# Expert token lists on four column strips of TensorE, and a new order of gather and scatters on GpSimd

## What is computed, cut to what matters

```python
capacity = max(1, int(Sz * CAP_FACTOR / E) + 1)          # 313 of 1250 tokens for each of 8 experts
scores = softmax(x @ router_w.T)
gate_vals, sel_idx = top_k(scores.T, capacity)
tokens = x[sel_idx]                                      # gather
h = gelu(tokens @ w1 + b1)                               # 1024 -> 512
y = h @ w2 + b2                                          # 512 -> 1024
out = zeros_like(x).at[sel_idx].add(y * gate_vals)       # scatter with add
x = x + out
```

## Time and profile before

| what | value |
|---|---|
| median of 3 runs | 1496.85 us (1491.33 to 1496.93) |
| the profiled execution: own time | 1494.7 us |
| its span in the profile | 1492.8 us |
| mean granted clock of TensorE | 0.982 of full |
| instructions | 28252 |
| PE, PEld, DVE, ACT, POOL busy | 1420.1, 727.0, 884.3, 545.5, 357.1 us |
| read from and written to memory | 118.40 MB, 41.94 MB |

### The profile page before, as it was taken

The page is one execution under the profiler, slowest core; times in us unless marked ns, Lnnn a source line. Parts: engine busy times, 40 slices in busy tenths (PEclk is TensorE's granted clock), DMA queues, the critical chain, the costliest instruction groups (busy, mean ns, idle before and its releaser), DMA issues.

```text
span 1492.8 us, 28252 instructions
## 1 busy us (share of the span) xinstructions
PE 1420.1 (95%) x8351; PEld 727.0 (49%) x8351; DVE 884.3 (59%) x1994; ACT 545.5 (37%) x758; POOL 357.1 (24%) x373
## 2 busy tenths in 40 slices
PE   6789999999999999999999999999999979999996
PEld 5344444545444444444654444446544436566653
DVE  7788888686987887541342222223337686576652
ACT  4578757373624543210111210001111124565651
POOL 4332320202201110000874002800012311343232
PEclk9999999999999999999999999999999987999998
DMA  7242010000166565553323443530046645789963
GB/s 282 43 86 51 8 43 14 28 0 28 70 193 168 162 167 174 144 144 108 130 72 88 98 111 113 183 105 22 0 130 197 196 177 205 217 249 273 281 164 57
DMA packets 156675, 185.96 MB, mean 125 GB/s; under 512 B 106172, under 2 KB 107659, under 8 KB 156600
## 3 DMA queue, kind: packets, MB, share of 16 engines
q1 hardware_dynamic: 144440, 143.07, 31.4%
q0 software_dynamic: 12160, 41.95, 11.0%
HBM read 118.40 MB, written 41.94 MB: 107 GB/s over the span
## 4 chain that ended last, share of the span: by engine, by line
PE 74%; DVE 11%; issue 6%; ACT 3%; DMA 2%; DVEq 1%; POOL 1%; ACTq 0%; SPq 0%; POOLq 0%
PE ps L1344 31%; PE ps L1412 11%; PE ps L1567 7%; PE ps L1587 6%; PE ps L1244 3%; PE ps L1246 3%; PE ps L1245 3%; PE ps L1175 2%; PE ps L1593 1%; PE ps L1555 1%; ACT th L1671 1%; DVE hm L2048 1%; PE ps L1273 1%; PE ps L1202 1%; PE ps L1236 1%
## 5 line engine op out<-in xcount | busy, mean ns | idle before, releaser
L1344 PE MATMUL ps<-wa,tb 128*128 128x512 f16 x960 | 212.2, 383 | 4.1 <-issue 4.1
L1412 PE MATMUL ps<-adj,nm 128*128 128x384 f16 (+2 forms) x960 | 169.6, 340 | 1.6 <-DVEq L2363 1.6
L1244 PE MATMUL ps<-gp,hop 128*128 (+1 forms) x400 | 151.6, 379 | 1.0 <-DVE gn L2122 1.0
L1344 PEld LDWEIGHTS ps<-wa,tb 128*128 (+1 forms) x960 | 94.1, 99 | 118.4 <-issue 9.4
L1245 PE MATMUL ps<-gp,hop 128*128 (+1 forms) x400 | 151.6, 379 | 0.0
L1246 PE MATMUL ps<-gp,hop 128*128 (+1 forms) x400 | 151.6, 379 | 0.0
L1412 PEld LDWEIGHTS ps<-adj,nm 128*128 x960 | 93.9, 98 | 77.2 <-issue 2.1
L1781 ACT ACTIVATE tb<-cx 128x384 f32 (+1 forms) x48 | 26.8, 559 | 276.8 <-DVE cx L2353 276.8
L1344 PE MATMUL ps<-wa,hop 128*128 128x512 f16 x480 | 105.3, 379 | 2.9 <-DVEq L2297 2.9
L1567 PE MATMUL ps<-tkT,wb 128*128 128x314 f16 x768 | 105.4, 300 | 0.8 <-ACT tkT L1854 0.8
L1344 PE MATMUL ps<-wb,hop 128*128 128x512 f16 x480 | 105.4, 383 | 0.0
(11 more groups left out here) (397 smaller groups left out, 2216.1 us busy)
## 6 DMA issues: line engine op xcount, KB each, us to landing
w_st<-in_ew SPq DMA_DIRECT2D x16, 2048.0 KB, 11.3
self_d<-cr SPq DMA_DIRECT2D x20, 512.0 KB, 3.0
cr<-self_d SPq DMA_DIRECT2D x20, 512.0 KB, 3.3
stage<-in_wn POOLq DMA_DIRECT2D x16, 512.0 KB, 3.8
x_d<-cr SPq DMA_DIRECT2D x10, 512.0 KB, 4.6
cx<-x_d SPq DMA_DIRECT2D x10, 512.0 KB, 4.0
cr<-x_d SPq DMA_DIRECT2D x10, 512.0 KB, 4.2
out<-cr SPq DMA_DIRECT2D x10, 512.0 KB, 3.5
```

The lines of the kernel that those rows point to most:

```text
L1244: pe.matmul(acc, wh, gh, start=(s_ == 0), stop=False, skip_group_check=True)
L1344: ins = pe.matmul(ps[:, b + c, :], lhs(part, k), w[:, w_, k, c * 512:(c + 1) * 512], start=(k == 0 and part == 0 and w_ == 0), stop=(last ...
L1412: ins = pe.matmul(ps[:, 6 + j, 0:n], nm[:, part, s_, bass.ds(f * P, P)], adj[:, s_, t0 * TP:t0 * TP + n], start=first, stop=(s_ == NT - 1 ...
```

## The change

Lists for experts 2 to 7 are computed the other way round. `tokg` of a tile (32 columns: 8 experts by 4 numbers) becomes the weights, on one of four 32-column strips of PE, and `selm` of the tile (384 columns) the moving data: 10 matmuls, tiles 0 to 3 on strips 0 to 3, tiles 4 to 7 again, tiles 8 and 9 on strips 0 and 1. The four strips' partial sums lie on 128 partitions of PSUM bank 0. ACT copies them as halfwords to `strip_lists` (`strips_out`), after it has applied the gates of chunk 0. PE's new `slots`, which stands in `ffn2` behind chunk 1, adds them up and turns them with 3 matmuls against a constant 0/1 matrix `strip_sum`. DVE's `lists` moves behind `out` 1. On POOL the gather moves from ahead of the scatter's chunk 0 to between its chunks 0 and 1. Two small POOL instructions at the program's start make `strip_sum`.

```diff
--- before.py
+++ after.py
@@ -260,6 +260,7 @@
         ones16 = sb("ones16", [P, P], F16)
         one32 = sb("one32", [1, 1], F32)
         sel = sb("sel", [P, 4, 8], F32)
+        strip_sum = sb("strip_sum", [P, 2, 4 * NE], F16)
         stage = sb("stage", [P, 2, 1024], F32)
         sc = sb("sc", [TP, NT, 8], F32)
         marks = sb("marks", [TP, NT, 2, 8], F16)
@@ -469,6 +470,8 @@
         selm = spare[:, 0:NT * 3 * P].rearrange("p (t n) -> p t n", t=NT)
         eb2 = spare[:, NT * 3 * P:NT * 3 * P + 4 * D].bitcast(F32).rearrange("p (j n) -> p j n", j=2)
         eb2t = spare[:, NT * 3 * P + 4 * D:NT * 3 * P + 6 * D].bitcast(F32).rearrange("p (j n) -> p j n", j=2)
+        strips_at = NT * 3 * P + 6 * D
+        strip_lists = spare[:, strips_at:strips_at + 3 * P]
         gE.close()
 
         w1b = wb[:].rearrange("p r (a k) n -> p r a (k n)", a=2)
@@ -541,6 +544,7 @@
         TURN_C, TURN_N, TURN_D = ([TURN_B[j] + 32 * (NT // 2) * n for j in range(2)] for n in (1, 2, 3))
         late = (NT - 2) // 2
         s_tick, s_wsh = sem("s_tick"), sem("s_wsh")
+        s_strips, s_stripped = s_candT, s_row
 
         def rows(ap, t, n=1):
 
@@ -685,6 +689,9 @@
             g.memset(pp[:, :, 16:32], 0.0)
             strips = ident[:].rearrange("p (q n) -> p q n", q=4)
             link(g.tensor_tensor(sel[:], strips[:, :, 0:8], strips[:, :, 8:16], ALU.add))
+            link(g.tensor_tensor(strip_sum[:], ident16[:, 0:64].rearrange("p (a n) -> p a n", a=2),
+                                 ident16[:, 64:128].rearrange("p (a n) -> p a n", a=2), ALU.add))
+            link(g.tensor_tensor(strip_sum[:, 0], strip_sum[:, 0], strip_sum[:, 1], ALU.add))
             g.sem_inc(s_rest, 1)
 
             uses = [0, 0]
@@ -862,9 +869,11 @@
                     g.indirect_dma_start(out=gx[0:n, j, c, :], out_offset=None, in_=h_d[:, :],
                                          in_offset=bass.IndirectOffsetOnAxis(ap=idx[0:n, j, c:c + 1], axis=0)).then_inc(s_gx[j][c], 16)
 
-            def scatter(i, j):
+            def scatter(i, j, between=none):
                 e = 2 * i + j
                 for c in range(3):
+                    if c == 1:
+                        between()
                     g.wait_ge(s_yg, 3 * e + c + 7)
                     g.sem_inc(s_tick, 1)
                     g.indirect_dma_start(out=out_d[:, :] if c < 2 else out_d.rearrange("n (o d) -> (n o) d", o=2),
@@ -875,9 +884,7 @@
                 g.sem_inc(s_scd, 1)
 
             def body(i, j, more):
-                if more:
-                    gather(i + 1, j)
-                scatter(i, j)
+                scatter(i, j, (lambda: gather(i + 1, j)) if more else none)
 
             for j in range(2):
                 g.wait_ge(s_h[j], 16 * (NT // 2))
@@ -1530,11 +1537,23 @@
                     return
                 pe.wait_ge(s_sel, e - 1)
                 pe.wait_ge(s_eev, 6 * e + 2)
+                pe.sem_inc(s_tick, 1)
+                for t in range(NT):
+                    q = t % 4
+                    ins = pe.matmul(ps[32 * q:32 * q + 32, 0, 0:3 * P], tokg[:, t].rearrange("p e n -> p (e n)"), selm[:, t, :],
+                                    start=(t < 4), stop=(t >= NT - 4), skip_group_check=True, tile_position=(0, 32 * q))
+                    if t >= NT - 4:
+                        ins.then_inc(s_strips, 1)
+
+            def slots(i, j):
+                e = 2 * i + j
+                pe.wait_ge(s_stripped, e)
+                pe.sem_inc(s_tick, 1)
+                of = strip_sum[:, 0].rearrange("p (e n) -> p e n", n=4)
                 for c in range(3):
-                    for t in range(NT):
-                        ins = pe.matmul(ps[:, 0, 4 * c:4 * c + 4], selm[:, t, c * P:(c + 1) * P],
-                                        tokg[:, t, e, :] if isinstance(e, int) else tile_of(tokg[:, t], e),
-                                        start=(t == 0), stop=(t == NT - 1))
+                    ins = pe.matmul(ps[:, 0, 384 + 4 * c:388 + 4 * c], strip_lists[:, c * P:(c + 1) * P],
+                                    of[:, e, :] if isinstance(e, int) else tile_of(of, e),
+                                    start=(c == 0), stop=(c == 2), skip_group_check=True)
                 ins.then_inc(s_lst, 1)
 
             def turn(i, j):
@@ -1569,7 +1588,7 @@
                                             stop=(k == KT - 1 and w_ == 1))
                     ins.then_inc(s_f1, 1)
 
-            def ffn2(i, j, between=none):
+            def ffn2(i, j, between=none, behind=none):
                 e = 2 * i + j
                 pe.wait_ge(s_wlo, 2 * e + 2)
                 pe.wait_ge(s_elo, 4 * e + 8)
@@ -1587,6 +1606,7 @@
                             ins = pe.matmul(ps[:, 6 + (j + o) % 2, :], hT[:, part, h, c * P:(c + 1) * P], half(h, w_, o),
                                             start=(n == 0), stop=(n == len(terms) - 1))
                         ins.then_inc(s_f2, 1)
+                behind()
                 pe.wait_ge(s_y, 5 * e + 5)
                 for n, (h, part, w_) in enumerate(terms):
                     for o in range(2):
@@ -1597,7 +1617,10 @@
 
             def body(i, j, more):
                 ffn1(i, j), turn(*after(i, j))
-                ffn2(i, j, (lambda: lists(i + 1, j)) if more else none)
+                if more:
+                    ffn2(i, j, lambda: lists(i + 1, j), lambda: slots(i + 1, j))
+                else:
+                    ffn2(i, j)
 
             def first():
                 pe.wait_ge(s_tok, 1)
@@ -1865,16 +1888,24 @@
                     s.wait_ge(s_gelu, 4 * e + h + 5)
                     s.activation(hT[:, 0, h, 0:FW], hb[:, h, 0:FW], ACT.Copy, scale=SA).then_inc(s_ehi, 1)
 
-            def gates(i, j):
+            def strips_out(i, j):
+                s.wait_ge(s_strips, 4 * (2 * i + j) - 3)
+                s.sem_inc(s_tick, 1)
+                s.activation(strip_lists, ps[:, 0, 0:3 * P], ACT.Copy).then_inc(s_stripped, 1)
+
+            def gates(i, j, between=none):
                 e = 2 * i + j
                 for c in range(3):
+                    if c == 1:
+                        between()
                     s.wait_ge(s_y, 5 * e + min(2 * c + 2, 5) + 2)
                     w_ = D if c < 2 else 512
                     s.activation(yb[:, c, 0:w_], yb[:, c, 0:w_], ACT.Copy, scale=sgate[:, j, c:c + 1]).then_inc(s_yg, 1)
 
             def body(i, j, more):
                 n = after(i, j)
-                high(*n, 0), hidden(i, j), turn(*n), high(*n, 1), gates(i, j)
+                high(*n, 0), hidden(i, j), turn(*n), high(*n, 1)
+                gates(i, j, (lambda: strips_out(i + 1, j)) if more else none)
 
             s.wait_ge(s_sc, NT)
             for j in range(2):
@@ -2535,7 +2566,8 @@
             def lists(i, j):
                 e = 2 * i + j
                 v.wait_ge(s_lst, e + 1)
-                link(v.tensor_copy(lst[:, j].rearrange("p c n -> p (c n)"), ps[:, 0, 0:12]))
+                at = 0 if isinstance(e, int) and e < 2 else 384
+                link(v.tensor_copy(lst[:, j].rearrange("p c n -> p (c n)"), ps[:, 0, at:at + 12]))
                 v.tensor_tensor(idx[:, j, :], lst[:, j, :, 0], pads[:], ALU.add).then_inc(s_idx, 1)
                 link(v.tensor_tensor(gate[:, j, :], lst[:, j, :, 1], lst[:, j, :, 2], ALU.add))
                 link(v.tensor_tensor(gate[:, j, :], gate[:, j, :], lst[:, j, :, 3], ALU.add))
@@ -2589,10 +2621,9 @@
             def body(i, j, more):
                 n = after(i, j)
                 low(*n, 0), hidden(i, j), turn(*n), keep(i, j)
-                out(i, j, 0)
+                out(i, j, 0), out(i, j, 1)
                 if more:
                     lists(i + 1, j)
-                out(i, j, 1)
                 if more == 2:
                     places(*after(i + 1, j))
                 out(i, j, 2), low(*n, 1)
```

## The result

The changed kernel takes 1510.08 us (median of 6 runs, 1505.85 to 1510.44); the kernel before, run beside it, 1495.90 (6 runs, 1491.33 to 1498.54). The ratio is 1.0090, 95% interval 1.0079 to 1.0102: slower by 0.9%. The prediction was 1503.0, range 1491.5 to 1513.0: the range holds the time, the point is 7.1 us low, and slower by over 0.5%, which is what happened, had only 0.38. The profiled execution took 1506.52 us with a span of 1504.7, so what the profile shows lacks 3.6 us of the median.

A forecast was written before the change was run, and what follows sets the result against it. PE, busy 95% of the span, was taken to bound the kernel. 1494.7 - 0.6 (lists) + 8.0 (five holes) + 0.5 (body 5) = 1502.6, say 1503 us; range 1491.5 to 1513.

The forecast's parts named there:

- The place and the chain: Late `idx`; gather and second scatter held by the two `low`; late all-landed signal; DVE's `out` late; hole before PE's chunk 1.
- The shift of the third scatter: On POOL: the third scatter ends at 1381.7 against 1374.48 before, 7.2 us later.
- The coin's edge: On POOL and DVE: the gather's third part and the first `low` meet within 0.1 us; taken as held.
- rival 1: Slack absorbs the delay, or the gather wins against `low`: no hole in PE, 1494.1 us; chance 0.34.
- cover: Slack before DVE's first `out` delays PE's chunk 1: 5.2 us here, 6.4 two bodies earlier, 5.8 taken for bodies 0 to 4.
- `strips_out` was free: ACT's copy, ready 1.85 us into chunk 1 of 5.27, with 3.4 us of cover: cost nothing.
- PE's part: Strips and `slots` take 0.65 us a list (0.58 to 0.72) against 0.75: -0.6 us for six.
- three of the old thirty: On PE: `slots`, 3 matmuls of 4 columns, priced like three of the old list matmuls: 0.075 us.
- The hole: PE idle ahead of chunk 1: delay 7.4 less cover 5.8, 1.6 us five times, 8.0; plus 0.5 for body 5.
- the last, which I had at 0.5: Body 5: no `places`, gather collides earlier, only one load follows; hole taken at 0.5 us.
- the 4.10: On POOL: the held scatter had spent 4.21 - 4.10, some 0.1 us, before it stopped.
- My case: The held DMAs outlast the cover and make holes in PE: total +7.9 us; chance 0.48, half given to slower.

The follow-up runs named there:

- first_landed: Changed kernel, but DVE's first `out` of an expert waits only for the first scatter, `out` 1 for all three: 1496.45 us, ratio 1.0005 to the kernel before.
- one_input: Changed kernel with both `low` of the expert bodies replaced by a product of one staged tile with zero: 1498.56 us, ratio 1.0014 to the kernel before.
- changed_again: The changed kernel run once more without edit, on one chip with the repeated moved-lists kernel: 1508.77 us, ratio 1.0085 to the kernel before.
- slots_mid: Changed kernel with `slots` between the halves of chunk 1 and DVE's `lists` between the halves of `out` 1: 1494.13 us, ratio 0.9996 to the kernel before.
- late_lists_again: Kernel before with its 30 list matmuls, `lists` behind `out` 1 and POOL's new order, run a second time: 1506.71 us, ratio 1.0075.
- late_lists: Kernel before with its 30 list matmuls kept, but DVE's `lists` behind `out` 1 and POOL's new order: 1503.23 us, ratio 1.0048.
- gather_first: Changed kernel with POOL's old order, the gather ahead of all three scatters: 1531.80 us, ratio 1.0248 to the kernel before.

## Why the prediction was right in its mechanism and low in its size

**The place and the chain were right.** The gather's third part and the second scatter at 5.0 and 4.8 us instead of 0.9 and 1.7; DVE's first `out` released by POOL; the gap ahead of the second chunk of an expert; none at `slots`; the two POOL instructions of the start free. The shift of the third scatter was worked out at 7.2 us and is 7.3. The coin's edge was one: in body 2 the gather's third part took 0.90 us, since it started ahead of `low`, and expert 3 had no hole: that is rival 1's variant. Body 1 is a third case. There 1.39 us lie between the two `low`, the second scatter starts 0.3 us ahead of the second one and takes 1.61 us, and the third is held (4.27 us from 1320.25); its issue ends 6.9 us later than before, but this is the body whose cover the prediction had at 6.4, and the hole is 0.3.

**`strips_out` was free, but by less than I wrote.** I had it ready 1.85 us into chunk 1, with 3.4 us of cover. In body 3 it is ready 4.07 us into chunk 1, because ACT's `high` stands ahead of the gate and waits until 1360.59 for its weights:

```profile
1360.59 3.62 ACT L1870 ACTIVATE wa<-w_st 128x4096 f16<-128x4096 f32 x1 [3.74 <-DMA w_st<-in_ew]
1365.16 0.47 ACT L1894 ACTIVATE adj<-ps 128x384 f16<-128x384 f32 x1
```

`slots` follows 5.19 us into the chunk, so 1.1 us of cover were left. In first_landed and one_input they ran out.

**PE's part: -0.6 was forecast, 0 measured.** The strips were well priced (0.60, forecast 0.50 to 0.64). The step that failed is `slots` at 0.075 us as "three of the old thirty". The three hold PE 0.15, 0.45 us more in six lists; the rest is that the strips came out at 0.60 and I had taken the middle of their range. I had priced matmuls in a run of thirty and applied that to three that stand alone between chunks. A round of the strips costs 0.20 us here (0.60 / 3) against 0.168 of the earlier trace rows, 0.10 more in all. The page TensorEngine Tiling (Array Packing) of the Trainium skill, section Key Properties, says that a change of mode drains TensorE; the 0.10 is compatible with that, and no run here separates the drain from the rest.

**The hole: 8.0 + 0.5 forecast, 8.5 measured, by luck in its spread.** The five holes that I had at 1.6 are 1.9, 0.3, 0, 2.5 and 2.4, 7.1 in sum; the last, which I had at 0.5, is 1.4. My own number for body 3 alone was 7.4 - 5.2 = 2.2 and it measured 2.5. Averaging the cover over the bodies made the late ones too small (1.6 for 2.5 and 2.4); the zero behind body 2 made it up again.

**The step that failed is one that is missing: a hole in PE was priced at its length.** Behind an idle stretch of about 2 us the granted clock can fall to half, and the next chunk then takes 1.6 to 1.7 us more; in the profiled run twice, 3.25 us. The earlier trace rows show PE without an idle entry, so the bodies before give no price. An earlier stage of the same trace does, behind 2.07 us of idle PE:

```profile
1088.63 11.56 PE L1344 MATMUL ps<-wa,tb 128*128 128x512 f16 x45 [2.07 <-issue]
1090.00:1092.00 2.00, 2.00 (x6) 0.62 (x5) 0.00 (x0) 0.00 (x0) 0.00 (x0) 0.50 0.60 87
```

The granted clock is 0.50 there too, with 6 matmuls in 2 us. The other idle stretch of 2.07 us, ahead of 791.09, is followed by 0.50 as well. So the price stood in the trace of the kernel before, and the prediction does not use it.

Forecast 1502.6, plus 0.6 for PE and 3.25 for the clock, with the holes at 8.5 as forecast, gives 1506.5: the profiled execution's own time is 1506.52. It lies 3.6 us under the median. Of this, 1.2 us is that the execution I summed from lies as much under the median of the kernel before (1494.7 against 1495.90). The rest varies from execution to execution: changed_again's own time is 1510.84, 4.3 us above the profiled one, with holes of 10.7 us in sum instead of 8.5, and its bodies start 1.7 us later (expert 0's chunk 0 at 1267.64 against 1265.90).

**One figure of the prediction stands in no row:** the 4.10 in "4.21 - 4.10 = some 0.1 us before it stopped". What it was to support, that a DMA met at its start is held, came out.

**The chances.** My case straddled +7.5 us and I gave half of it to slower. With the clock in the sum it lies at +11.8, past that line, and slower should have had most of the weight. The term left out (1.6 us behind a hole) was as large as the hole that I had priced.

## What to carry to other kernels

A step moved from an idle stretch to a busy one has to be followed on every engine: here 7 us of delay came from an index list that was ready 5.8 us later in the body, because a gather that just missed its gap met one long VectorE instruction, and the scatter behind it the next. With the list 2.6 us earlier (slots_mid) nothing was lost. Where one wait stands for several transfers, ask which one the waiting instruction needs: waiting for the first scatter alone gave back the whole loss. And a hole in TensorE can cost twice, once as time and once as the clock behind it. Both prices may already stand in the trace of the kernel before, in another stage.

## What the runs showed of the hardware

- **Two long VectorE instructions back to back hold two indirect DMAs.** The first is let go 0.77 us behind the end of the one `low` although the next starts at once (1375.92 against a DMA that ends at 1376.73); the second waits out the whole of the other. VectorE is not slowed: 4.41 and 4.42 us, as in the earlier trace rows.
- **The half clock is not certain behind a given hole.** By PE's idle entries, chunks of some 7.0 us stand behind 1.31 (late_lists_again), 1.75 and 1.84 (late_lists), 2.13 and 2.38 us (changed_again) and behind all six idle entries of gather_first, 3.0 to 6.3 us, and chunks of 5.35 behind 1.81 (the changed kernel), 1.80 and 2.79 us (changed_again). What decides between them stays open.
- **The signal trails the last scatter's issue as far as before.** In body 3 it is 8.6 us (1392.3 - 1383.7) against 8.3, over bodies 0 to 5 it is 7.0 to 8.6 against 7.1 to 8.8, though the scatter starts later, when the loads should have been further along; I had expected that part to shrink, and it did not. DMA share was 1.06 and 0.97 in the windows 1390 to 1392 and 1392 to 1394, around the signal.
